# A macaron layer on one core: attention scores as three fp32r products, and four pieces of work moved around them

## The chip, the core and the metric

The kernel runs on one core of a Trainium2 chip. The core has TensorE (matrix products, with its own stream of weight loads), VectorE, ScalarE, GpSimd, and SyncE, which only issues transfers. Each engine takes its instructions in the order in which the program lists them, and waits on semaphores that other engines raise. The metric is the time of one execution in microseconds of the device; lower is better.

## What is computed

The input is `x` of 16 batches x 512 rows x 256 columns. A layer is three residual parts: half a feed-forward network, attention with 16 heads of 64, half the same feed-forward network.

```
x = x + 0.5 * ffn(layernorm(x))
x = x + attention(layernorm(x))
x = x + 0.5 * ffn(layernorm(x))

attention: q, k, v = split(x @ w_qkv); per head
  sim = (q * 64**-0.5) @ k.T - |i - j| * slope(head); causal mask; softmax
  out = sim @ v, heads side by side, @ w_out + b_out
ffn: gelu(x @ w1 + b1) @ w2 + b2
```

## The kernel before

Weights stay in SBUF. Every matmul but two kinds is made of three fp32r products: each operand is split into a high part (the value written as fp32r) and a low part (the value less its high part, written as fp32r), and `hi*hi + hi*lo + lo*hi` is summed in PSUM. The two kinds that use plain fp32 operands are the scores `q @ k.T` and the product of the probabilities with `v`. A plain fp32 matmul shows as two MATMUL records.

Work goes batch by batch. The attention of a batch goes by pairs of heads, c = 0 to 7; I call the pass for one pair a step, and the sixteen records of its scores (before) a block. A block has four parts by row block i, in the order 3, 2, 0, 1 (`QORDER`), of 128(i+1) key columns, and in each part two heads, which use the upper and the lower 64 rows of TensorE. In a step c from 2 on, the engines do this:

- **TensorE**: the block of pair c; the projections k and q of pair c+1 (six products of 512 columns each); a tile of v (twelve products of 256 columns); the product with v of pair c-2 (`values`). In step 6 there are two tiles of v and then the transposes of the next batch's first layer norm (`ln_transpose`, two units of four).
- **ScalarE**: copies of k, q and v out of PSUM (`proj_copy`), the exponentials (`exps`), the copy of `values`.
- **VectorE**: `biased` adds the distances and takes the row minimum, part by part; `inverse` takes reciprocals of the row sums, once for the parts 3 and 2 and once for 0 and 1; `turned` transposes the probabilities of pair c-1 in place, in a large and a small half.
- **GpSimd**: `normalise` multiplies the probabilities by the reciprocals (eight multiplies in two groups of four); then it issues 5 of the 16 transfers that spread the transposed probabilities over the partitions (`spread`). SyncE issues the other 11.

Steps 0 and 1 of a batch stand in `begin`. There TensorE also has the second feed-forward network of the batch before: its up tiles, and its four down tiles `dn(2, b-1, t)`, which VectorE adds to x (`add3`), one by one. Steps are not synchronised otherwise: order on each engine, semaphores, and PSUM banks set the times. Banks are given in turn from a set named by `among`; before a bank is used again, TensorE waits for whoever reads what it held (`bank_free`). Banks 0 to 5 hold scores, bank 5 those of part 1 of the second head. Two places matter here. In step 1, the projection q of pair 2 takes the bank of down tile 1, so it waits for `add3(b-1, 1)`. In step 6 the second unit of transposes takes bank 5, so it waits for `biased(b, 6, 1)`:

```
ln_transpose(1, b + 1, 0)
among[0] = (5,)
ln_transpose(1, b + 1, 1)
```

The next batch's first layer norm has, on VectorE, four `stats` (each a statistics and an aggregate instruction) and a `variance` in step 4, and four `normal` in step 5, all behind the `inverse` at the end of the step; GpSimd takes the power (`power`) in between. `bias` on GpSimd adds a bias to x.

## Time and profile before

| | before |
|---|---|
| time, median of 3 runs (lowest, highest) | 2186.82 us (2186.59, 2187.15) |
| time of the profiled execution | 2185.37 us |
| its span, first to last instruction | 2183.6 us |
| mean granted TensorE clock | 0.995 |
| TensorE matmuls busy | 98% of the span |
| VectorE, ScalarE, GpSimd busy | 69%, 57%, 48% |

The span is what the instructions of the profile cover; 1.8 us of the profiled execution lie around it. Busy shares are of the whole span; matmuls overlap each other in the records, so their starts tell more than their lengths.

### The profile page before, as it was taken

How to read it: one execution, taken by the hardware profiler on the slowest of the kernel's cores; microseconds unless marked ns; L12 is line 12 of the kernel's file. 1: busy time of each engine (PE TensorE's matmuls, PEld its weight loads, DVE VectorE, ACT ScalarE, POOL GpSimd, SP SyncE). 2: the span in 40 equal slices, each digit the busy share in tenths (PEclk: the TensorE clock that was granted, in tenths of full speed). 3: DMA queues.
4: the chain of work that ended last, by engine and by line, in shares of the span. 5: the costliest groups of instructions: out<-in, count | busy, mean ns of one | idle time of the engine just before them, and what ended most of it. 6: DMA issues, size and time to landing. Idle time of an engine off the chain costs nothing.

```text
span 2183.6 us, 41803 instructions
## 1 busy us (share of the span) xinstructions
PE 2138.1 (98%) x14720; PEld 1737.8 (80%) x14720; DVE 1501.8 (69%) x4014; ACT 1234.2 (57%) x3096; POOL 1052.7 (48%) x1770
## 2 busy tenths in 40 slices
PE   7999999999999999999999999999999999999988
PEld 6688787877878788787887878778787787878867
DVE  6766767667676676766768676676766767667664
ACT  5745646466464664736557364564646647465471
POOL 1744627346273553726537174462734537255371
PEclk9999999999999999999999999999999999999998
DMA  3422505234051331514325052250513405143151
GB/s 131 131 73 75 139 1 160 54 90 125 17 149 49 109 104 35 153 27 123 92 62 137 16 141 73 78 135 1 162 52 92 121 23 151 42 115 99 34 146 34
DMA packets 109985, 193.91 MB, mean 89 GB/s; under 512 B 34512, under 2 KB 53200, under 8 KB 109776
## 3 DMA queue, kind: packets, MB, share of 16 engines
q1 hardware_dynamic: 88816, 137.95, 22.5%
q0 software_dynamic: 20480, 52.47, 9.7%
q8 instruction: 117, 1.92, 0.4%
q10 hardware_dynamic: 480, 0.82, 0.1%
q14 instruction: 92, 0.75, 0.1%
HBM read 14.95 MB, written 8.39 MB: 11 GB/s over the span
## 4 chain that ended last, share of the span: by engine, by line
PE 88%; POOL 4%; ACT 4%; DVE 2%; issue 1%; SPq 1%; DMA 0%; DVEq 0%; POOLq 0%
PE ps L302 86%; POOL P L982 3%; PE ps L356 2%; ACT P L629 2%; DVE P L821 1%; ACT L629 1%; SPq L245 1%; POOL PT L245 0%; ACT qk L589 0%; DVE x L768 0%; DMA raw<-in_L_ffn_w 0%; DVE gl L739 0%; DMA PT<-P 0%; DVE P L813 0%; DVE rs L804 0%
## 5 line engine op out<-in xcount | busy, mean ns | idle before, releaser
L982 POOL TENSOR_SCALAR P<-P,rs 128x512 f32<-128x512 f32 (+3 forms) x1024 | 538.5, 543 | 442.9 <-DVE rs L804 439.6
L629 ACT ACTIVATE P<-P,mx 128x512 f32<-128x512 f32 (+3 forms) x1024 | 562.1, 552 | 195.1 <-DVE mx L813 194.9
L245 POOL DMA_DIRECT2D PT<-P x640 | 321.6, 508 | 242.5 <-DVE P L821 228.4
L821 DVE STREAM_TRANSPOSE P<-P 128x1792 f32<-128x1792 f32 (+1 forms) x256 | 374.1, 1486 | 16.2 <-POOL P L982 15.7
L302 PE MATMUL ps<-PT,v 128*64 128x256 f32 (+1 forms) x3072 | 307.5, 349 | 8.5 <-DMA PT<-P 8.4
L302 PE MATMUL ps<-qk 64*128 64x512 f32 (+3 forms) x2048 | 311.0, 443 | 0.7 <-ACT qk L589 0.7
L302 PE MATMUL ps<-w2h,gh 128*128 128x256 f32 x1024 | 292.7, 286 | 0.4 <-DVE gl L739 0.4
L302 PE MATMUL ps<-w2l,gh 128*128 128x256 f32 x1024 | 289.7, 283 | 0.0
L302 PE MATMUL ps<-w2h,gl 128*128 128x256 f32 x1024 | 289.5, 283 | 0.0
L302 PEld LDWEIGHTS ps<-PT,v 128*64 128x64 f32 x3072 | 204.8, 137 | 105.7 <-issue 16.0
L589 ACT ACTIVATE qk<-ps 128x512 f32<-128x512 f32 x256 | 152.7, 597 | 229.9 <-PE ps L302 229.9
L813 DVE CUSTOM_DVE_ANT_1 P<-ps,dist 128x384 f32<-128x384 f32 (+2 forms) x768 | 272.3, 414 | 0.0
L607 ACT ACTIVATE gt<-ps,b1c 128x512 f32<-128x512 f32 x256 | 172.8, 688 | 164.4 <-PE ps L302 130.8
L302 PEld LDWEIGHTS ps<-qk 64*128 64x128 f32 x2048 | 166.2, 187 | 114.9 <-issue 75.8
L813 DVE CUSTOM_DVE_ANT_0 P<-ps,dist 128x512 f32<-128x512 f32 x256 | 165.7, 684 | 122.2 <-PE ps L302 122.2
L768 DVE TENSOR_TENSOR x<-ps,x 128x256 f32<-128x256 f32 x192 | 80.5, 419 | 238.4 <-PE ps L302 236.7
L970 POOL TENSOR_TENSOR rstd<-ve,mhalf 128x4 f32<-128x4 f32 x48 | 62.9, 1310 | 363.2 <-DVE ve L754 363.2
L302 PE MATMUL ps<-xth,wqh 128*128 128x512 f32 x512 | 211.7, 413 | 5.9 <-DVE x L768 4.4
L302 PEld LDWEIGHTS ps<-w2h,gh 128*128 128x128 f32 x1024 | 196.0, 191 | 10.2 <-issue 7.5
L302 PE MATMUL ps<-xtl,wqh 128*128 128x512 f32 x512 | 201.1, 393 | 0.0
L302 PE MATMUL ps<-xth,wql 128*128 128x512 f32 x512 | 199.8, 390 | 0.0
L302 PEld LDWEIGHTS ps<-w2l,gh 128*128 128x128 f32 x1024 | 196.0, 191 | 1.8
(83 smaller groups left out, 4392.4 us busy)
## 6 DMA issues: line engine op xcount, KB each, us to landing
PT<-P SPq DMA_DIRECT2D x1398, 80.0 KB, 2.6
PT<-P POOLq DMA_DIRECT2D x640, 80.0 KB, 2.7
x<-in_L_attn_x SPq DMA_DIRECT2D x16, 512.0 KB, 4.2
out_y<-x SPq DMA_DIRECT2D x15, 512.0 KB, 3.2
raw<-in_L_ffn_w SPq DMA_DIRECT2D x2, 512.0 KB, 5.9
raw<-in_L_ffn_w SPq DMA_DIRECT2D x1, 1024.0 KB, 8.8
rawq<-in_L_attn_w_qkv SPq DMA_DIRECT2D x1, 1024.0 KB, 6.6
rawk<-in_L_attn_w_qkv SPq DMA_DIRECT2D x1, 1024.0 KB, 8.7
```

Source lines behind the costliest of these rows:

```text
L245: e.dma_start(PT[c % 2][32 * m:32 * m + 32, g, :], P[c % 3][32 * g:32 * g + 32, m, :]).then_inc(landed.sem, 16)
L302: return e.matmul(out, lhsT, rhs, start=first, stop=last)
L356: last = e.transpose(dst[:, col:col + 128], xn[:, t, k * 128:(k + 1) * 128], ident[:, :])
L589: e.activation(dst, src, ACT.Copy).then_inc(s_pc.sem, 1)
L607: e.activation(gt[m % 3][:, :], bank_of(("up", f, b, m)), ACT.Gelu, bias=b1c[:, m:m + 1]).then_inc(s_gl.sem, 1)
L629: e.activation(p, p, ACT.Exp, bias=mx[:, r, i:i + 1], scale=-1.0, accum_out=sm[:, r, i:i + 1]).then_inc(s_ex.sem, 1)
L768: e.tensor_tensor(xb[b % 2][:, t, :], bank_of(use)[:, 0:D], xb[b % 2][:, t, :], ALU.add).then_inc(events.sem, 1)
L813: e.tensor_tensor_reduce(out=p_block(c, h, i), in0=score_block(h, i).rearrange("p (m n) -> p m n", m=4), in1=dist[:, :, 128 - 32 * (i + 1) ...
L821: e.transpose(p, p).then_inc(s_tr.sem, 1)
L970: e.tensor_tensor(rstd[:, L - 1, :], ve[:, L - 1, :], mhalf[:, :], ALU.pow).then_inc(s_pw.sem, 1)
L982: e.tensor_scalar(p, p, rs[:, 2 * (c % 2) + h, i:i + 1], 1.0, ALU.mult, ALU.mult).then_inc(s_nz.sem, 1)
```

## The change

- The copies of q and k go to an fp32 buffer `qkf` (for pair 0 of a batch one place, for all others a second). Behind the copy of q, ScalarE writes the high parts of both in one instruction of 1024 elements a partition (`qkh`, one buffer). VectorE's new `qk_lo` writes the low parts, also 1024 elements, over `qkf`. A block then waits for `qk_lo` in place of the copy of q, and each of its parts is three fp32r products for each head. The keys are stored in the order in which the block reads them.
- `qk_lo` of pair c+1 stands in step c behind `biased` of part 0 and ahead of part 1; for pair 0 behind the last `normal` of the batch, for pair 1 behind the gelu splits, for pair 2 behind `add3(b-1, 2)`.
- The next batch's `stats` go to steps 2 and 3 with `variance` in 3, `power` to step 3, and the four `normal` to steps 4 and 5, two each, behind `qk_lo` and ahead of `biased` of part 1.
- `add3(b-1, 1)` goes ahead of `turned(b, 0, 1)`. The copy of k or q now waits for the block just before, not the one two before.
- GpSimd's last `bias` of a batch waits for `qk_lo` of the next batch's pair 0.
- GpSimd issues 6 of the 16 transfers of a spread, SyncE 10; in the last two spreads ScalarE issues 4 in place of 5.

```diff
--- before.py
+++ after.py
@@ -62,7 +62,9 @@
 
     R = at[0]
     QK, V, PP, PT_AT, GT = R, R + 8192, R + 16384, R + 47104, R + 67584
-    qk = [place(f"qk{i}", [128, 2, T], F32, QK + 4096 * i) for i in range(2)]
+    qkh = place("qkh", [128, 2, T], F32R, QK)
+    qkf = [place(f"qkf{i}", [128, 2, T], F32, a) for i, a in enumerate((PP + 10240, QK + 4096))]
+    qkl = [place(f"qkl{i}", [128, 2, T], F32R, a) for i, a in enumerate((PP + 10240, QK + 4096))]
     v = [place(f"v{i}", [128, NT, 4, DH], F32, V + 4096 * i) for i in range(2)]
     P = [place(f"P{i}", [128, 4, GW], F32, PP + 16 * GW * i) for i in range(3)]
     PT = [place(f"PT{i}", [128, 4, GW], F32, PT_AT + 16 * GW * i) for i in range(2)]
@@ -169,6 +171,8 @@
     s_ex = Signal("ex_done", per_block)
     s_pc = Signal("proj_copied", proj)
     s_oa = Signal("out_copied", pairs)
+    s_kh = Signal("qk_hi", pairs)
+    s_kl = Signal("qk_lo", pairs)
     s_lh = Signal("lh_done", units)
     s_gl = Signal("gl_done", hidden)
     s_oh = Signal("oh_done", outs)
@@ -197,12 +201,12 @@
     s_fh = Signal("fh_done", range(NC))
     s_fl = Signal("fl_done", range(NC))
     s_yt = Signal("y_tile_out", range(NT), 16)
-    s_la = {c: Signal(f"spread_last_act{c}", [(NB - 1, c)], 5 * 16) for c in (NC - 2, NC - 1)}
+    s_la = {c: Signal(f"spread_last_act{c}", [(NB - 1, c)], 4 * 16) for c in (NC - 2, NC - 1)}
     s_ls = {c: Signal(f"spread_last_sp{c}", [(NB - 1, c)], 6 * 16) for c in (NC - 2, NC - 1)}
     s_x = Signal("x_in", list(B), 16)
     s_y = Signal("y_out", list(B), 16)
-    s_pt = [Signal(f"spread{i}", [(b, c) for b, c in pairs if c % 3 == i], 11 * 16) for i in range(3)]
-    s_pp = [Signal(f"spread_pool{i}", [(b, c) for b, c in pairs if c % 3 == i], 5 * 16) for i in range(3)]
+    s_pt = [Signal(f"spread{i}", [(b, c) for b, c in pairs if c % 3 == i], 10 * 16) for i in range(3)]
+    s_pp = [Signal(f"spread_pool{i}", [(b, c) for b, c in pairs if c % 3 == i], 6 * 16) for i in range(3)]
     names = ["w1a", "w1b", "b1", "w2", "b2", "wq", "wk", "wv", "wout", "bout"]
     s_w = {n: Signal("in_" + n, [0], 16) for n in names}
 
@@ -230,8 +234,8 @@
         return DH ** -0.5 / SLOPE[h]
 
     GROUPS = [(m, g) for m in range(4) for g in range(4)]
-    SPREAD_SP, SPREAD_POOL = GROUPS[:11], GROUPS[11:]
-    LAST_SP, LAST_ACT, LAST_POOL = GROUPS[:6], GROUPS[6:11], GROUPS[11:]
+    SPREAD_SP, SPREAD_POOL = GROUPS[:10], GROUPS[10:]
+    LAST_SP, LAST_ACT = GROUPS[:6], GROUPS[6:10]
     LAST = (NC - 2, NC - 1)
 
     def spread(e, b, c, groups, landed):
@@ -424,17 +428,20 @@
                 last.then_inc(s_pj.sem, 1)
 
             def scores(b, c):
-                e.wait_ge(s_pc.sem, s_pc.at((b, ("q", c))))
+                e.wait_ge(s_kl.sem, s_kl.at((b, c)))
+                lo = qkl[min(c, 1)]
                 for i in QORDER:
-                    w = 128 * (i + 1)
                     for h in range(2):
                         if i != 0:
                             bank_free(h + {3: 0, 2: 2, 1: 4}[i])
                             held[h + {3: 0, 2: 2, 1: 4}[i]] = ("scores", b, c, 0 if i == 2 else i, h)
-                        hs = slice(64 * h, 64 * h + 64)
-                        keys = qk[c % 2][hs, 1, 0:w].rearrange("p (j m s) -> p m j s", m=4, s=32)
-                        mm(score_block(h, i), qk[c % 2][hs, 0, i * 128:i * 128 + 128], keys,
-                           True, True).then_inc(s_qk.sem, 1)
+                    for n, (q, k) in enumerate(((qkh, qkh), (qkh, lo), (lo, qkh))):
+                        for h in range(2):
+                            hs = slice(64 * h, 64 * h + 64)
+                            keys = k[hs, 1, :].rearrange("p (m n) -> p m n", m=4)[:, :, 0:32 * (i + 1)]
+                            last = mm(score_block(h, i), q[hs, 0, i * 128:i * 128 + 128], keys, n == 0, n == 2)
+                            if n == 2:
+                                last.then_inc(s_qk.sem, 1)
 
             def values(b, c):
                 pv = bank_for(("values", b, c))
@@ -583,10 +590,17 @@
                 else:
                     kind, c = tile
                     n = pairs.index((b, c))
-                    if n >= 2:
-                        e.wait_ge(s_qk.sem, s_qk.at((*pairs[n - 2], QORDER[-1], 1)))
-                    dst = qk[c % 2][:, 0 if kind == "q" else 1, :]
+                    if n >= 1:
+                        e.wait_ge(s_qk.sem, s_qk.at((*pairs[n - 1], QORDER[-1], 1)))
+                    if kind == "q":
+                        dst = qkf[min(c, 1)][:, 0, :]
+                    else:
+                        dst = qkf[min(c, 1)][:, 1, :].rearrange("p (m j s) -> p j m s", m=4, s=32)
+                        src = src.rearrange("p (j m s) -> p j m s", m=4, s=32)
                 e.activation(dst, src, ACT.Copy).then_inc(s_pc.sem, 1)
+                if tile[0] == "q":
+                    e.wait_ge(s_pc.sem, s_pc.at((b, tile)))
+                    e.activation(qkh[:, :, :], qkf[min(c, 1)][:, :, :], ACT.Copy).then_inc(s_kh.sem, 1)
 
             def ln_hi(L, b, u):
                 e.wait_ge(s_lt.sem, s_lt.at((L, b, u)))
@@ -815,6 +829,11 @@
                         in1=dist[:, :, 128 - 32 * (i + 1):128], scale=-SLOPE[2 * c + h],
                         scalar=BIG, op0=ALU.add, op1=ALU.min, accum_out=mx[:, r, i:i + 1]).then_inc(s_tt.sem, 1)
 
+            def qk_lo(b, c):
+                e.wait_ge(s_kh.sem, s_kh.at((b, c)))
+                n = min(c, 1)
+                residue(qkl[n][:, :, :], qkf[n][:, :, :], qkh[:, :, :]).then_inc(s_kl.sem, 1)
+
             def turned(b, c, half):
                 e.wait_ge(s_nz.sem, s_nz.at((b, c, 1, 2 if half else 1)))
                 p = P[c % 3][:, :, HALF[half]]
@@ -825,19 +844,22 @@
                     biased(b, 0, i)
                 if b > 0:
                     gelu_split(2, b - 1, range(NM))
+                qk_lo(b, 1)
+                if b > 0:
                     add3(b - 1, 0)
                 inverse(b, 0, 1)
                 biased(b, 1, 3)
                 biased(b, 1, 2)
                 inverse(b, 0, 0)
-                turned(b, 0, 1)
                 if b > 0:
                     add3(b - 1, 1)
+                turned(b, 0, 1)
                 turned(b, 0, 0)
                 biased(b, 1, 0)
                 biased(b, 1, 1)
                 if b > 0:
                     add3(b - 1, 2)
+                qk_lo(b, 2)
                 inverse(b, 1, 1)
                 if b > 0:
                     add3(b - 1, 3)
@@ -863,17 +885,23 @@
                         turned(b, c - 1, 0)
                     else:
                         turned(b, c - 1, 0)
-                        for i in QORDER[1:]:
+                        for i in QORDER[1:3]:
                             biased(b, c, i)
+                        if c + 1 < NC:
+                            qk_lo(b, c + 1)
+                        if more and c in (4, 5):
+                            normal(1, b + 1, 2 * c - 8)
+                            normal(1, b + 1, 2 * c - 7)
+                        biased(b, c, QORDER[3])
                     inverse(b, c, 1)
-                    if more and c == 4:
+                    if more and c == 2:
                         e.wait_ge(s_x.sem, s_x.at(b + 1))
-                        for t in range(NT):
-                            stats(1, b + 1, t)
+                        stats(1, b + 1, 0)
+                        stats(1, b + 1, 1)
+                    if more and c == 3:
+                        stats(1, b + 1, 2)
+                        stats(1, b + 1, 3)
                         variance(1, b + 1)
-                    if more and c == 5:
-                        for t in range(NT):
-                            normal(1, b + 1, t)
                     if more and c == 6:
                         inverse(b, c, 0)
                         ln_lo(1, b + 1, 0)
@@ -933,6 +961,7 @@
             for u in range(2):
                 ln_lo(2, 0, u)
             split_weight_lo("wv")
+            qk_lo(0, 0)
             e.wait_ge(s_id.sem, s_id.at("dist"))
             for b in B:
                 more = b + 1 < NB
@@ -956,6 +985,8 @@
                 variance(3, b)
                 for t in range(NT):
                     normal(3, b, t)
+                if more:
+                    qk_lo(b + 1, 0)
                 ln_lo(3, b, 0)
                 ln_lo(3, b, 1)
             gelu_split(2, NB - 1, range(NM))
@@ -990,7 +1021,7 @@
                         for h in range(2):
                             normalise(b, c, h, i)
                     if b + 1 < NB:
-                        if c == 4:
+                        if c == 3:
                             power(1, b + 1)
                         if c == NC - 2:
                             bias(1, b + 1)
@@ -1022,6 +1053,8 @@
                     power(2, b + 1)
                     bias(2, b + 1)
                 power(3, b)
+                if b + 1 < NB:
+                    e.wait_ge(s_kl.sem, s_kl.at((b + 1, 0)))
                 bias(3, b)
```

## Rows read from the trace of the kernel before

**Rows 1.** The page, busy time of each engine
```profile
PE 2138.1 (98%) x14720; PEld 1737.8 (80%) x14720; DVE 1501.8 (69%) x4014; ACT 1234.2 (57%) x3096; POOL 1052.7 (48%) x1770
```

**Rows 2.** Timeline, TensorE, one step (start us, us, engine, instruction)
```profile
1010.75 2.43 PE L302 MATMUL ps<-qk 64*128 64x512 f32 x16
1013.10 0.50 PE L302 MATMUL ps<-xth,wqh 128*128 128x512 f32 x1
1013.44 0.40 PE L302 MATMUL ps<-xtl,wqh 128*128 128x512 f32 x1
...
1015.96 0.28 PE L302 MATMUL ps<-wqh,xth 128*128 128x256 f32 x1
...
1017.27 0.28 PE L302 MATMUL ps<-wqh,xtl 128*128 128x256 f32 x1
1017.48 2.38 PE L302 MATMUL ps<-PT,v 128*64 128x256 f32 x24
1019.79 1.13 PE L302 MATMUL ps<-qk 64*128 64x512 f32 x4
```

**Rows 3.** Timeline, TensorE's weight loads, start of one block of scores
```profile
1001.69 0.30 PEld L302 LDWEIGHTS ps<-qk 64*128 64x128 f32 x4
```

**Rows 4.** Groups of instructions by form (count, busy us, mean ns, idle before)
```profile
L739 DVE TENSOR_TENSOR ol<-o,oh 128x1024 fp32r<-128x1024 f32 x60 | 71.9, 1219 | 44.1 <-ACT oh L618 44.1
...
L618 ACT ACTIVATE oh<-o 128x1024 fp32r<-128x1024 f32 x60 | 60.2, 1052 | 40.2 <-PE ps L302 39.7
...
L748 DVE BATCH_NORM_STATS2 st<-x 128x6 f32<-128x256 f32 x192 | 80.0, 417 | 9.3 <-DMA x<-in_L_attn_x 4.9
```

**Rows 5.** Timeline, VectorE, the same step as rows 2
```profile
1011.91 0.69 DVE L813 CUSTOM_DVE_ANT_0 P<-ps,dist 128x512 f32<-128x512 f32 x1 [2.61 <-PE ps L302]
...
1013.13 0.17 DVE L804 RECIPROCAL rs<-sm 128x4 f32<-128x4 f32 x1
1013.22 2.87 DVE L821 STREAM_TRANSPOSE P<-P 128x1792 f32<-128x1792 f32 x2
1016.02 0.52 DVE L813 CUSTOM_DVE_ANT_1 P<-ps,dist 128x384 f32<-128x384 f32 x1
...
1017.37 0.42 DVE L813 CUSTOM_DVE_ANT_1 P<-ps,dist 128x256 f32<-128x256 f32 x1
...
1018.06 0.17 DVE L804 RECIPROCAL rs<-sm 128x4 f32<-128x4 f32 x1
```

**Rows 6.** Timeline, GpSimd, the same step
```profile
1013.40 1.62 POOL L982 TENSOR_SCALAR P<-P,rs 128x128 f32<-128x128 f32 x4 [0.64 <-DVE rs L804]
1016.67 2.50 POOL L245 DMA_DIRECT2D PT<-P  x5 [1.65 <-DVE P L821]
1019.21 2.47 POOL L982 TENSOR_SCALAR P<-P,rs 128x512 f32<-128x512 f32 x4
```

**Rows 7.** Timeline, ScalarE, the same step
```profile
1016.15 0.60 ACT L589 ACTIVATE qk<-ps 128x512 f32<-128x512 f32 x1 [0.76 <-PE ps L302]
```

**Rows 8.** Timeline, VectorE, step 5: first two tiles normalised
```profile
1036.24 0.71 DVE L762 TENSOR_SCALAR xn<-x,mv,rstd 128x256 f32<-128x256 f32 x2
```

**Rows 9.** Timeline, TensorE, step 1: where it waits
```profile
993.68 0.39 PE L302 MATMUL ps<-xth,wql 128*128 128x512 f32 x1
994.36 0.50 PE L302 MATMUL ps<-xth,wqh 128*128 128x512 f32 x1 [0.29 <-DVE x L768]
```

**Rows 10.** Timeline, VectorE, the add that it waits for
```profile
993.92 0.39 DVE L768 TENSOR_TENSOR x<-ps,x 128x256 f32<-128x256 f32 x1
```

**Rows 11.** Timeline, TensorE, down tile 0 and the block behind it
```profile
984.22 0.28 PE L302 MATMUL ps<-w2h,gh 128*128 128x256 f32 x1
...
987.18 0.70 PE L302 MATMUL ps<-qk 64*128 64x512 f32 x2
```

**Rows 12.** Timeline, TensorE, step 6: start of its block, and the transposes
```profile
1037.88 2.43 PE L302 MATMUL ps<-qk 64*128 64x512 f32 x16
...
1045.97 1.04 PE L356 MATMUL ps<-ident,xn 128*128 128x128 f32 x8
```

## Prediction

> **What bounds the kernel now.** I read the page first: TensorE is busy 98% of the span, the next engine 69% [rows 1]. So a microsecond is won only where TensorE gets less to do, and is lost wherever it is made to wait. Then I read TensorE's timeline over one step [rows 2]: block of scores, two projections, a tile of v, `values`, and the next block, 9.04 us later (1019.79 - 1010.75), each tile starting right behind the last. Then the timelines of the other engines over the same step [rows 5 to 7], to see how late each may be before TensorE notices. All times below are counted from the start of the step's block.
>
> **The block gets shorter.** Now it takes 13.10 - 10.75 = 2.35 us, to the start of the projection [rows 2]. For the new one I need the price of an fp32r product. From the second product of the projections to the first of v are 11 products of 512 columns: 2.52/11 = 0.229 us each. From 15.96 to 17.27 are 11 products of 256 columns: 0.119 each [rows 2]. So 0.11 us more for 256 columns more; 384 columns by that line cost 0.174. For 128 columns the line gives 0.065, but a load of weights goes with each product, and where it is not hidden it adds 0.34 - 0.229 = 0.11 (13.10 to 13.44). A product can't be faster than its load, so I take 0.12 for 128 columns too. Two heads: four loads of a block start and end within 0.30 us [rows 3], where four in series would take 0.44 and more, so the two halves of the array load and run side by side, and I count each pair of products once. Three products for each of the four parts: 3 x (0.229 + 0.174 + 0.119 + 0.12) = 1.93; the first load is bare, 0.11; the drain before the next tile is 17.48 - 17.27 - 0.12 = 0.09. New block 2.13 us, 0.22 to 0.23 saved (I use 0.23, from unrounded starts). 16 batches x 8 blocks = 128: **29.4 us** saved if nothing else changes.
>
> Bounds of this price. Below: the slope alone (0.11 per 256 columns) is 0.218 for 512, so 0.011 of each product is a fixed part; if products on half of the array don't have it, and 128 columns cost the bare load of 0.11, the block is about 1.96, 0.40 saved. Above: no fp32r product of fewer than 256 columns is in the trace; if one of 128 costs as much as one of 512, the block is 2.13 + 3 x 0.109 = 2.46, 0.10 lost. I take the middle, as the nearest row is the product of 256 columns.
>
> **What a block now waits for.** ScalarE's copy of q starts at 5.40 and takes 0.60 [rows 7]. All of this comes 0.23 earlier. Then the high parts: 1024 elements, as ScalarE's `oh` copy, 1.05; then the low parts, as VectorE's `ol`, 1.22 [rows 4]. For each handover I take 0.04, an estimate (the add of 993.92 ends at 994.31, TensorE starts again by 994.36 [rows 9, 10]). High parts ready: 5.17 + 0.60 + 0.04 + 1.05 + 0.04 = 6.90; low parts 8.12. The next block is due at 9.04 - 0.23 = 8.81: hidden behind v and `values`, with 0.7 to spare, if VectorE is there on time.
>
> VectorE has the time: its step runs from 11.91 to 18.06 and a reciprocal, 6.25 us [rows 5], and `qk_lo` adds 1.14 (records overlap by 0.08: 1017.37 to 1018.06 is two of 0.42 in 0.69). ScalarE too: it idles 0.76 before q [rows 7], and more elsewhere. But the two run in a ring with GpSimd, and here is the cost.
>
> **The ring.** `normalise` starts 0.27 after the reciprocal (13.13 to 13.40 [rows 5, 6]) and its first four multiplies take 2.47; then the turning, 2.80 to the next instruction; parts 2 and 0, 1.35 (16.02 to 17.37); now `qk_lo` 1.14; in steps 4 and 5 now two `normal`, 0.32 each [rows 8]; part 1, 0.69; the reciprocal again. With `normal` the ring takes 0.27 + 2.47 + 0.04 + 2.80 + 1.35 + 1.14 + 0.64 + 0.69 = 9.40 against a step of 8.81. A second ring, turning 2.87, wake-up and five issues to 19.21 (3.12 after the turning's end at 16.09), one more issue 0.50, multiplies 2.47, takes 9.0. Before, the rings took 7.6 and 8.5 and TensorE led at 9.04.
>
> Followed through: in steps 2 and 3 the second ring loses 0.2 a step, and the moved `stats` (0.42 each and their aggregates [rows 4]) end about where the next part 3 begins. In step 4 `qk_lo` starts at 7.0, the reciprocal at 7.0 + 1.14 + 0.64 + 0.69 = 9.47, the multiplies end at 12.21, and the turning of step 5 starts at 12.25 - 8.81 = 3.44, where VectorE alone would be at 2.3. In step 5 `qk_lo` starts at 3.44 + 2.80 + 1.35 = 7.59 and ends at 8.81, when the block is due: 0.05 lost. The reciprocal is at 10.06, the turning of step 6 at 3.98, `qk_lo` at 8.13, part 1 of the second head ends at 10.03.
>
> **The new wait.** In step 6 the second unit of transposes needs bank 5, so that very part. It came at 1045.97 + 4 x 0.11 - 1037.88 = 8.53 [rows 12], now 8.30. TensorE goes on at 10.03 + 0.04 + 0.11 (a bare load) = 10.18: **1.89 us** of waiting, in 15 batches, with the 0.05 of step 5: 29.1 us. Behind it nothing is late: all that follows in step 7 hangs on TensorE or on VectorE, which are pushed alike.
>
> **Step 1.** TensorE waits before q of pair 2, as `add3(b-1, 1)` stands behind a turning: 994.36 - 993.68 - 0.23 = 0.45, and a bare load, 0.11 [rows 9, 10]. With the add first this goes: the add can start when its tile is ready, about 0.8 before q. But block 1 has only a down tile as cover: copy of q 0.20 after that tile's start at 984.22 (as in rows 2 and 7: 15.96 to 16.15), then 0.60 + 0.04 + 1.05 + 0.04 + 1.22 + 0.04 = 987.41, where the block began at 987.18 [rows 11]: 0.23 lost. Net 0.33 x 15 = 5.0 saved. The exponentials of pair 0 start a microsecond later; the two down tiles before block 2 cover it.
>
> **The first batch** has no down tiles there. Block 1 gets 1.05 + 1.22 + 0.08 = 2.35 more behind q, block 0 about 1.6 more (its tile of v covers the rest): 4.0 lost. Free of charge: GpSimd's `bias`, which stands idle at that place until the first multiplies of the batch; one issue fewer for SyncE, since `values` starts without a wait [rows 2]; the strided copy of the keys, as those of v are no slower. The wait for the next batch's x comes two steps sooner; `stats` stand last in step 2, so only an x that lands later than their place there would hold up VectorE, and the next part 3 with it.
>
> **Sum.** 29.4 + 5.0 - 29.1 - 4.0 = 1.3 us saved of the profiled execution's 2185.37 (span 2183.6 and 1.8 around it), so 2184.1; the median of the runs lies 1.45 above that execution, so **2185.5**. No change, by a measurement that can tell 0.2% (4.4 us).
>
> **Rivals.**
> - *Cheaper products* (0.40 a block). 51.2 + 5.0 - 4.0 saved, but the step is then 8.64, the rings lag sooner, `qk_lo` in step 5 stops the block by 0.5 and step 6 waits 2.1: 15 x 2.6 = 38. Saves 13.9: 2173. For it: the slope. Against it: the fixed part is in every fp32r row there is. The Trainium skill (TensorE: Matmul & The Clock Gate, "Wait — 56ns, not 53.3ns?") gives a fixed part of some 2.5 ns per matmul, which speaks for this rival; the trace has 11 for fp32r.
> - *The rings don't add up*, because the waits overlap better than I chain them. Then `qk_lo` starts in step 6 when the high parts are ready, at 6.90, part 1 ends at 8.80, and the wait is 0.65: 29.4 + 5.0 - 9.8 - 4.0 = 20.7 saved, 2166. Against it: each link is a measured length.
> - *Short products dear*, the other side: one of 128 columns costs what one of 512 does. 128 x 0.10 = 12.8 lost in blocks; the longer step cuts the wait of step 6 to 1.13, 17.0 lost; with + 5.0 and - 4.0, 28.8 lost: 2215.6. It decides from about 0.145 us for 128 columns on. For it: no row excludes it.
> - *Loads not hidden*: each product of a head waits for its own load. The twelve pairs of products stream for 3 x (0.229 + 0.174 + 0.119 + 0.065) = 1.76 and load for 12 x 0.11 = 1.32; with the drain 3.17, 0.82 lost: 105 in blocks, some 9 in step 6: about 2300. Against it: in the projections a load per product is hidden [rows 2]. The Trainium skill (TensorE: Matmul & The Clock Gate, "The mechanism" of packing) says that a load overlaps running matmuls only where their row groups differ; by that rule this rival would hold, and the projections' 0.119 for 256 columns speaks against it.
>
> **How the numbers follow.** The forecast has 0.50; its own range is the wait of step 6 to 0.4 us, 15 x 0.4 = 6: 2179.5 to 2191.5. Cheaper products 0.18, rings that don't add up 0.12, short products dear 0.10, loads 0.06, anything else 0.04. Faster by over 0.2% (below 2182.4): the second and third, and a quarter of the first: 0.42. Slower: dear products, loads, a little of the rest: 0.22. Same: 0.36. The range 2165 to 2212 leaves out the loads, half of the dear products, a third of the rings' case and some of the rest, about 0.18.
>
> **What would show it.** Blocks of 2.13 us; products of 128 columns 0.12 apart; the wait before the second unit of transposes in step 6, put down to VectorE's part 1, at 1.9 us; the turning of steps 5 and 6 beginning at 3.4 and 4.0; no wait before q in step 1 and 0.2 before block 1. I am wrong if the block is not near 2.13, if the transposes don't wait, or if `values` or an up tile does.

## The result, and the profile after

The changed kernel takes 2235.31 us (median of 4 runs, 2233.0 to 2237.1), the kernel before 2186.86: a ratio of 1.0216 with an interval of 1.0204 to 1.0229. The forecast was 2185.5, "no change", with a range up to 2212; the kernel is slower by 48.5 us.

The page of the changed kernel, busy time by engine and then the chain that ended last (the chain of work followed back from the last instruction). The first answers to [rows 1]; the second fence has the chain of the kernel before:

```profile
PE 2121.1 (95%) x15744; PEld 1808.2 (81%) x15744; DVE 1651.8 (74%) x4142; ACT 1368.4 (61%) x3224; POOL 1121.4 (50%) x1898
...
PE 53%; DVE 25%; POOL 5%; DMA 5%; issue 4%; ACT 4%; SPq 4%; DVEq 0%; POOLq 0%; ACTq 0%
```

```profile
PE 88%; POOL 4%; ACT 4%; DVE 2%; issue 1%; SPq 1%; DMA 0%; DVEq 0%; POOLq 0%
```

TensorE is busy 17 us less, but the chain now leaves it for 47% of its length, where it was 12% before. First what went as forecast, a block and its step on TensorE's timeline (batch 4, step 2; it answers to [rows 2]):

```profile
617.77 0.50 PE L306 MATMUL ps<-qkh 64*128 64x512 f32 x2
618.11 0.40 PE L306 MATMUL ps<-qkl,qkh 64*128 64x512 f32 x2
618.34 0.39 PE L306 MATMUL ps<-qkh,qkl 64*128 64x512 f32 x2
618.57 0.34 PE L306 MATMUL ps<-qkh 64*128 64x384 f32 x2
...
619.16 0.28 PE L306 MATMUL ps<-qkl,qkh 64*128 64x128 f32 x2
619.27 0.28 PE L306 MATMUL ps<-qkh,qkl 64*128 64x128 f32 x2
...
619.88 0.50 PE L306 MATMUL ps<-xth,wqh 128*128 128x512 f32 x1
...
624.26 2.38 PE L306 MATMUL ps<-PT,v 128*64 128x256 f32 x24
626.58 0.50 PE L306 MATMUL ps<-qkh 64*128 64x512 f32 x2
```

The block takes 619.88 - 617.77 = 2.11 us (forecast 2.13), the step 8.81. A pair of products of 512 columns costs 0.23, one of 128 columns 0.11. So the gain in the blocks is there, and something else took it. I took the start of every block from the traces; a step is the distance to the next block. Means over batches 1 to 14, in us, for the kernels of this study (the forecast's row is worked out from the typical steps of before and the terms of the prediction):

| kernel | step 0 | 1 | 2 | 3 | 4 | 5 | 6 | 7 | batch | median time |
|---|---|---|---|---|---|---|---|---|---|---|
| before | 19.05 | 14.52 | 9.05 | 9.05 | 9.10 | 9.09 | 11.37 | 52.10 | 133.32 | 2186.86 |
| forecast | 19.05 | 13.72 | 8.81 | 8.81 | 8.81 | 8.86 | 13.02 | 51.85 | 132.93 | 2185.5 |
| **after** | 19.05 | 13.68 | 8.81 | 9.41 | 10.14 | 9.81 | 13.04 | 52.34 | 136.27 | 2235.31 |
| 1 layer norm back | 19.05 | 13.68 | 8.81 | 9.23 | 8.82 | 9.87 | 14.71 | 52.28 | 136.44 | 2240.04 |
| 2 variance of two inputs | 19.05 | 13.68 | 8.81 | 9.36 | 9.99 | 9.81 | 13.13 | 52.30 | 136.12 | 2233.28 |
| 3 variance later | 19.05 | 13.68 | 8.81 | 9.53 | 8.95 | 9.70 | 13.11 | 52.32 | 135.15 | 2217.28 |
| 4 add3 alone | 19.06 | 13.93 | 9.06 | 9.29 | 9.09 | 9.05 | 11.40 | 52.09 | 132.96 | 2180.94 |
| 5 qk_lo(7) late | 19.06 | 13.68 | 8.81 | 9.58 | 8.94 | 9.66 | 12.84 | 52.33 | 134.90 | 2213.30 |
| 6 inverse first | 19.06 | 13.68 | 8.81 | 9.29 | 8.95 | 9.47 | 12.86 | 52.34 | 134.46 | 2208.39 |
| 7 five issues | 19.05 | 13.68 | 8.81 | 9.94 | 9.15 | 9.19 | 12.85 | 52.32 | 135.00 | 2215.84 |
| 8 layer norm a step later | 19.05 | 13.68 | 8.81 | 9.14 | 8.82 | 9.18 | 12.50 | 52.45 | 133.63 | 2197.59 |
| 9 the same, 8 columns | 19.05 | 13.68 | 8.81 | 9.03 | 8.82 | 9.16 | 12.42 | 52.33 | 133.31 | 2193.75 |
| 10 k first | 19.06 | 13.68 | 8.81 | 9.25 | 10.14 | 9.80 | 13.03 | 52.35 | 136.11 | 2236.76 |
| 11 inverse and v | 19.06 | 13.68 | 8.81 | 9.17 | 8.82 | 9.16 | 12.59 | 52.54 | 133.83 | 2194.16 |
| 12 the same, five issues | 19.06 | 13.68 | 8.81 | 9.58 | 8.81 | 8.81 | 12.37 | 52.26 | 133.37 | 2193.26 |
| 13 part 1 first in 6 | 19.05 | 13.68 | 8.80 | 9.53 | 8.81 | 8.83 | 12.15 | 52.55 | 133.41 | 2192.63 |
| 14 x a step later | 19.06 | 13.68 | 8.81 | 8.90 | 8.82 | 8.98 | 12.15 | 52.54 | 132.92 | 2187.46 |
| 15 x later, six issues | 19.05 | 13.68 | 8.81 | 8.93 | 8.82 | 9.20 | 12.29 | 52.52 | 133.29 | 2192.59 |
| 16 both v first | 19.06 | 13.68 | 8.81 | 8.92 | 8.84 | 8.93 | 11.26 | 54.67 | 134.17 | 2205.12 |
| 17 after, step 6 alone | 19.06 | 13.68 | 8.81 | 9.38 | 10.01 | 9.80 | 11.95 | 53.69 | 136.37 | 2237.17 |
| 18 second v between | 19.05 | 13.68 | 8.81 | 8.90 | 8.95 | 9.02 | 11.42 | 53.28 | 133.10 | 2189.52 |

Steps 0 to 2 and 6 of "after" are as forecast. Steps 3, 4 and 5 are longer by 0.60, 1.33 and 0.95, step 7 by 0.49. Three single steps stand out of these means: step 7 of batch 2 takes 54.56 where most take 52.12, step 5 of batches 7 and 12 takes 12.02 and 11.80 where most take 9.46. In or just before each of them GpSimd stood some 2.7 us between two issues, for nothing that the profile shows (batch 7, GpSimd):

```profile
1053.97 1.08 POOL L249 DMA_DIRECT2D PT<-P  x2 [0.65 <-DVE P L840]
1057.76 0.99 POOL L249 DMA_DIRECT2D PT<-P  x2 [2.70 <-issue]
```

The other batches lose as well, and what was late there is on VectorE's timeline (batch 4, from the end of step 2 to part 3 of step 4):

```profile
628.18 0.43 DVE L762 BATCH_NORM_STATS2 st<-x 128x6 f32<-128x256 f32 x1 [1.51 <-DMA x<-in_L_attn_x]
...
629.32 0.69 DVE L827 CUSTOM_DVE_ANT_0 P<-ps,dist 128x512 f32<-128x512 f32 x1
...
637.66 0.18 DVE L764 BATCH_NORM_AGGREGATE mv<-st 128x2 f32<-128x6 f32 x1
637.88 1.76 DVE L768 TENSOR_SCALAR ve<-mv 128x4 f32<-128x4 f32 x1
639.54 0.68 DVE L827 CUSTOM_DVE_ANT_0 P<-ps,dist 128x512 f32<-128x512 f32 x1
```

First, the stats wait 1.51 us for x, so part 3 of step 3 begins 629.32 - 626.58 = 2.74 us behind its block, where batch 15, which has no next layer norm, has 1.0. SyncE's queue says why x is late: its load waits until the store of y has landed.

```profile
619.90 0.58 SPq L268 DMA_DIRECT2D out_y<-x  x1
623.08 0.38 SPq L260 DMA_DIRECT2D x<-in_L_attn_x  x1
623.56 5.83 SPq L249 DMA_DIRECT2D PT<-P  x9
```

Second, the variance, an instruction over 4 elements, takes 1.76 us and ends as GpSimd's four multiplies do, 637.12 + 2.49 = 639.61 (GpSimd's timeline):

```profile
637.12 2.49 POOL L1013 TENSOR_SCALAR P<-P,rs 128x512 f32<-128x512 f32 x4
```

So part 3 of step 4 begins 3.48 behind its block. Behind it ScalarE has its exponentials and then the copy of k, and every later link of the step moves with it. (Beside GpSimd's multiplies the variance isn't always so slow; the last section has its row in the kernel before.) The list of waits shows where TensorE feels it (us in total, times, longest):

```profile
PEld ps L306 <- DVE qkl L753: 37.1, 63, 3.5
PEld ps L306 <- ACT qkf L600: 30.4, 27, 2.1
...
DVE st L762 <- DMA x<-in_L_attn_x: 22.7, 14, 4.7
```

### The profile page after: what moved, and what is told of

The parts are those of the page before. It is cut to its first block, busy times and chain, and to the rows that moved or that the text cites. A ratio compares the mean times of both kernels' runs of the same rounds, so it can differ in the third digit from the quotient of the medians.

```text
span 2233.1 us, 44380 instructions
## 1 busy us (share of the span) xinstructions
PE 2121.1 (95%) x15744; PEld 1808.2 (81%) x15744; DVE 1651.8 (74%) x4142; ACT 1368.4 (61%) x3224; POOL 1121.4 (50%) x1898
## 4 chain that ended last, share of the span: by engine, by line
PE 53%; DVE 25%; POOL 5%; DMA 5%; issue 4%; ACT 4%; SPq 4%; DVEq 0%; POOLq 0%; ACTq 0%
PE ps L306 52%; DVE P L840 10%; DVE P L827 6%; POOL P L1013 4%; DVE qkl L753 4%; SPq L249 4%; DMA x<-in_L_attn_x 3%; DMA out_y<-x 2%; ACT qkh L603 2%; PE ps L360 2%; DVE xn L776 1%; ACT qkf L600 1%; DVE st L762 1%; POOL PT L249 1%; ACT P L643 1%
## 5 line engine op out<-in xcount | busy, mean ns | idle before, releaser
L249 POOL DMA_DIRECT2D PT<-P x768 | 388.7, 512 | 227.3 <-DVE P L840 208.6
L827 DVE CUSTOM_DVE_ANT_1 P<-ps,dist 128x384 f32<-128x384 f32 (+2 forms) x768 | 278.3, 415 | 0.2 <-PE ps L306 0.2
L600 ACT ACTIVATE qkf<-ps 128x512 f32<-128x512 f32 x256 | 149.7, 593 | 158.1 <-PE ps L306 158.1
L753 DVE TENSOR_TENSOR qkl<-qkf,qkh 128x1024 fp32r<-128x1024 f32 x128 | 156.6, 1223 | 63.1 <-ACT qkh L603 61.5
L306 PE MATMUL ps<-qkh 64*128 64x512 f32 (+3 forms) x1024 | 179.4, 347 | 24.0 <-DVE qkl L753 24.0
L306 PEld LDWEIGHTS ps<-w2h,gl 128*128 128x128 f32 x1024 | 196.1, 192 | 0.0
L643 ACT ACTIVATION_READ_ACCUMULATOR P<-P,mx 128x1 f32 x1024 | 193.8, 189 | 0.0
```

What stands on the lines that cost most here:

```text
L249: e.dma_start(PT[c % 2][32 * m:32 * m + 32, g, :], P[c % 3][32 * g:32 * g + 32, m, :]).then_inc(landed.sem, 16)
L306: return e.matmul(out, lhsT, rhs, start=first, stop=last)
L600: e.activation(dst, src, ACT.Copy).then_inc(s_pc.sem, 1)
L643: e.activation(p, p, ACT.Exp, bias=mx[:, r, i:i + 1], scale=-1.0, accum_out=sm[:, r, i:i + 1]).then_inc(s_ex.sem, 1)
L753: return e.tensor_tensor(dst, src, hi.bitcast(F32), ALU.subtract)
L827: e.tensor_tensor_reduce(out=p_block(c, h, i), in0=score_block(h, i).rearrange("p (m n) -> p m n", m=4), in1=dist[:, :, 128 - 32 * (i + 1) ...
```

## The experiments

Theory T: the moved layer norm makes VectorE late in steps 2 to 5. Theory R: the ring through `qk_lo`, the multiplies, the turning and six issues is the loss wherever the layer norm stands. Intervals of the ratio to the kernel before are in brackets.

**1. Layer norm back.** `stats` and `variance` in step 4, `normal` in step 5, behind the inverse, as before the change (the cut shows the new places; the lines at the old ones go).

```
-                    if more and c == 2:   # stats 0, 1; c == 3: stats 2, 3, variance
+                    if more and c == 4:   # wait for x, stats 0 to 3, variance
+                    if more and c == 5:   # normal 0 to 3
```

> The changed kernel with the next batch's layer norm back at its old place: the four stats and the variance behind the inverse of step 4, the four normals behind the inverse of step 5, the power in step 4. The three products, the order of b2's adding, the 10 and 6 issues and add3 stay. Theory T (the moved layer norm makes part 3 late on VectorE, and by ScalarE's order k and the v tile): steps 3 and 4 fall from 9.41 and 10.14 to 8.81 and about 9.0, step 5 (9.81) to about 9.5, step 6 stays at about 13.0, so some 2 us a batch, 30 in all: about 2205 us. Theory R (the ring through qk_lo and GpSimd's issues is the loss wherever the layer norm stands): steps 4 and 5 stay near 10 and the time within 8 us of 2235.

2240.04 (1.0225 to 1.0255). Neither: step 4 came down as T has it and step 3 in part (9.23), but step 6 rose to 14.71. Beside `qk_lo` the old place costs as much as the new one. VectorE and GpSimd in step 5 of batch 4:

```profile
657.03 3.79 DVE L776 TENSOR_SCALAR xn<-x,mv,rstd 128x256 f32<-128x256 f32 x4
```

```profile
657.55 2.48 POOL L1010 TENSOR_SCALAR P<-P,rs 128x512 f32<-128x512 f32 x4
```

The first normal takes 0.38, the second 2.84: it ends when the fourth multiply does. So another instruction is held as the variance was.

**2 and 3. Two ways around the hold.** Run 2 computes the variance by another form at the same place; run 3 moves it.

```
-                e.tensor_scalar(ve[:, L - 1, :], mv[:, L - 1, :, 1], EPS, None, ALU.add)
+                e.scalar_tensor_tensor(ve[:, L - 1, :], mhalf[:, :], -2.0 * EPS, mv[:, L - 1, :, 1], ALU.mult, ALU.add)
```

```
                         biased(b, c, 3)
+                        if more and c == 4:
+                            variance(1, b + 1)
                         inverse(b, c - 1, 0)
```

> The changed kernel with the variance computed by another form of instruction at the same place: mhalf (-0.5) times -2 EPS plus the variance, from two tiles, in place of one tile plus a constant. Theory T1 (a tensor_scalar on VectorE that starts while GpSimd multiplies is held until GpSimd ends, and the other form is not): its duration falls from 1765 ns to about 0.2 us, part 3 of step 4 begins at about 1.9 us behind its block in place of 3.48, step 4 falls from 10.14 to about 9.0 to 9.4, and the time to some 2218 to 2225 us. Theory T2 (any small instruction is held there): the duration stays near 1.77 us and the time at 2235.

> The changed kernel with the variance moved from behind stats 2 and 3 in step 3 to behind part 3 of step 4, where GpSimd has ended its multiplies and only issues DMAs or waits. If GpSimd's multiplies hold it (T1, T2 alike), it takes about 0.2 us there, part 3 of step 4 begins some 1.5 us sooner, and the time falls to some 2218 to 2225 us. If the variance is slow for a reason of its own, it takes 1.77 us there as well, in front of the inverse and the turning, and the time is at 2235 or above.

2233.28 (1.0193 to 1.0228) and 2217.28 (1.0117 to 1.0150). The variance by its tile in run 2, then in run 3 (count, shortest/median/longest ns):

```profile
L770 DVE SCALAR_TENSOR_TENSOR ve<-mhalf,mv x48: 161/164/1736, 7.0 to 2197.5; 128x4 f32<-128x4 f32 x48
```

```profile
L768 DVE TENSOR_SCALAR ve<-mv x48: 169/170/596, 7.1 to 2184.9; 128x4 f32<-128x4 f32 x48
```

The form with two inputs is held just as long. Behind part 3 of step 4 GpSimd hasn't ended its multiplies yet, though the expectation has it so: the variance still meets the last of the four and ends with it, but that makes it 0.6 at the most. Step 4 falls by 1.19, which is 16.7 in 14 batches, and the time by 18.0 against 2235.31 (the four runs spread from 2211.5 to 2220.3). So that hold alone is about a third of the loss.

**4. `add3` alone**, in the kernel before.

```
+                if b > 0:
+                    add3(b - 1, 1)
                 turned(b, 0, 1)
-                if b > 0:
-                    add3(b - 1, 1)
```

> The kernel before with one edit: add3(b-1,1) ahead of turned(b,0,1) in step 1, scores as one product. If the wait of 0.56 us that [rows 9] shows in step 1 goes and nothing takes its place, step 1 falls from 14.52 to about 13.96 in 15 batches: 2178.4 us (8.4 less). If the turning that is later by one addition is itself waited for (by the DMAs and the values of step 1), step 1 stays at 14.52 and the time at 2186.8.

2180.94 (0.9955 to 0.9981): the fastest kernel of the study. Step 1 gains 0.59 as forecast, but step 3 gives 0.24 of it back: in batch 2 it takes 10.04, since `values` start at 350.25, behind a copy of v on ScalarE that ends at 350.20. Why that copy is late in some batches I didn't follow.

**5 to 7. One link of the ring each**, from run 3: `qk_lo(b, 7)` behind the inverse of step 6; the inverse ahead of part 1; 11 and 5 issues in place of 10 and 6.

```
-                        if c + 1 < NC:
+                        if c + 1 < NC and not (more and c == NC - 2):
                             qk_lo(b, c + 1)
...
+                    if more and c == NC - 2:
+                        qk_lo(b, NC - 1)
```

```
+                        inverse(b, c, 1)
                         biased(b, c, QORDER[3])
-                    inverse(b, c, 1)
```

```
-    SPREAD_SP, SPREAD_POOL = GROUPS[:10], GROUPS[10:]
+    SPREAD_SP, SPREAD_POOL = GROUPS[:11], GROUPS[11:]
```

> The kernel of the later variance (2217.3), with qk_lo(b,7) in step 6 behind part 1 and the inverse in place of ahead of part 1; the score block that needs it comes 13 us behind that of step 6. Step 6 (13.11) holds two waits of the next batch's transposes: the first for the v copy that ScalarE has behind the exponentials of part 2, the second for the bank that part 1 gives back. If only the second goes by qk_lo(7), step 6 falls by about 0.5 to 12.6 and the time to about 2209; if the whole 1.7 that step 6 has gained over before is qk_lo(7)'s, step 6 falls to about 11.4 and the time to 2192; if the low parts of the last pair are then late for block 7 or hold up the next batch's low parts, the time stays at 2217 or rises.

> The kernel of the later variance (2217.3), with the inverse of parts 3 and 2 ahead of part 1 on VectorE, so that GpSimd's multiplies start some 0.8 us sooner behind qk_lo. Theory R1 (the chain qk_lo, normals, part 1, inverse, multiplies, turning, parts 2 and 0, qk_lo sets steps 5 and 6): step 5 (9.70) falls to about 9.0 and the lag into step 6 is less, 0.7 to 1.2 us a batch, 2200 to 2207 us. Theory R2 (GpSimd's own chain of six issues, four multiplies and the turning sets them): 9.0 us a step stays, and since the inverse was early enough there, the time stays within 4 us of 2217.

> The kernel of the later variance (2217.3), with the issues of the turned tiles shared 11 and 5 as in the kernel before, in place of 10 and 6. By R2, GpSimd's chain shortens by one issue of 0.49 us: steps 5 and 6 fall by 0.3 to 0.5 each, about 2205 us. By R1, GpSimd waits for VectorE anyway: within 4 us of 2217, or some us above if SP's eleventh issue makes the values late.

2213.30 (1.0107 to 1.0137), 2208.39 (1.0084 to 1.0114) and 2215.84 (1.0114 to 1.0147), against 2217.28. The inverse first gave 8.9, with step 5 at 9.47, between the expectation's theories R1 and R2. `qk_lo(b, 7)` late gave 4.0, which the spread of run 3 doesn't tell from nothing, though step 6 fell by 0.27. Five issues shortened steps 5 and 6 by 0.51 and 0.26, as R2 has it, lengthened steps 3 and 4 by 0.41 and 0.20, and left the time as it was.

**8. Layer norm a step later**, from run 5: stats in steps 3 and 4, variance behind part 3 of step 5, normals in 5 and 6.

```
-                        if more and c in (4, 5):   # normal 2c-8, 2c-7
+                        if more and c in (5, 6):   # normal 2c-10, 2c-9
-                    if more and c == 2:            # wait for x, stats 0, 1; c == 3: 2, 3
+                    if more and c == 3:            # wait for x, stats 0, 1; c == 4: 2, 3
```

> The kernel with qk_lo(7) late, with each part of the next batch's layer norm one step later: stats 0 and 1 in step 3, stats 2 and 3 in step 4, the variance behind part 3 of step 5, the normals in steps 5 and 6, the power in step 4's turn on GpSimd. If the wait for x in step 2 is what makes steps 3 and 4 long, step 3 falls from 9.5 to about 8.85 and the time by about 10 us against the kernel with qk_lo(7) late. If VectorE's added work itself (2.1 us of stats over two steps with 0.7 us to spare in each) makes them long, step 4 and 5 take over what step 3 gives up, and the time stays within 4 us of it; if the normals in step 6 are late for the transposes, step 6 grows by about 1 us and the time by 15.

2197.59 (1.0036 to 1.0066), 15.7 below run 5. Steps 4 and 5 are at 8.81 in most batches, step 3 is still long in some, and step 6 fell by 0.34 though it now has two normals in it.

**9. What the layer norm's length is worth**, from run 8: from batch 1 on, the statistics and the four normals take 8 of 256 columns; the rest of that computation is left out. (Cut; `normal` has the same edit.)

```
+                n = 8 if L == 1 and b > 0 else D
-                e.bn_stats(st[:, L - 1, t, :], xb[b % 2][:, t, :])
+                e.bn_stats(st[:, L - 1, t, :], xb[b % 2][:, t, 0:n])
```

> The kernel with each part of the layer norm a step later (2197.6), with the next batch's stats and normals computed over 8 of 256 columns (that part of the computation is left out), the same instructions in the same places. What VectorE's time in them is worth: by theory T (VectorE, with some 8.1 of 8.81 us taken in each step, has no room for the layer norm's 3.9 us and hands the lag on into step 6) step 6 falls from 12.50 to about 11.5 and the time by 12 to 20 us, to 2178 to 2186. By theory R (the low parts and GpSimd's chain alone make step 6 long) step 6 stays above 12.2 and the time at 2193 or more.

2193.75 (1.0020 to 1.0042): step 6 at 12.42. So once the layer norm stands a step later, its length is not what makes step 6 long, as R has it. A stats with its aggregate still takes 0.27 us there and a normal 0.29, so this took only some 1.5 us of VectorE's time from a batch.

**10. k first**, from the changed kernel.

```
-                    exps(b, c, 3)
                     if c + 1 < NC:
                         proj_copy(b, ("k", c + 1))
+                    exps(b, c, 3)
```

> The changed kernel with one edit in ScalarE's order: from step 2 on, the copy of k(c+1) ahead of the exponentials of part 3 of step c in place of behind them. If a late part 3 reaches TensorE through ScalarE's order (theory T's middle link), the waits of the v tile for k's copy (0.8 to 1.5 us in steps 3 and 4) go: step 4 falls from 10.14 to 9.3 to 9.6, step 3 by some 0.3, and the time to about 2220 to 2227. If the late qk_lo holds the next block just as long, steps 3 and 4 stay as they are and the time within 4 us of 2235; if the exponentials are now late for the multiplies, it rises.

2236.76 (1.0215 to 1.0246): step 4 stays at 10.14, so the first reading missed. The order on ScalarE is where TensorE's wait is booked, but without it `qk_lo`, itself behind the late turning, holds the next block just as long: in batch 4 the wait of 1.12 for the copy goes and the block of step 5 waits 1.22 for `qk_lo`.

**11 and 12. Inverse and v**, from run 8: the inverse first, and in step 6 ScalarE's copy of the first v tile ahead of the exponentials of part 2; run 12 with five issues.

```
+                    if more and c == NC - 2:   # step 6: first v tile here
                     exps(b, c, 2)
-                    for tile in steps_v(b, c)[:1]:
```

> The kernel with each part of the layer norm a step later (2197.6), with the inverse of parts 3 and 2 ahead of part 1 as in the run with the inverse first, and in step 6 the copy of the v tile ahead of the exponentials of part 2 on ScalarE. The inverse shortens VectorE's chain by 0.77 us a round, so the turning of step 6 starts nearer 2.8 than 3.5 us; the v copy takes the first of step 6's two waits (1.27 us) away, and then the second, for the bank of part 1, sets the end. Step 6 falls from 12.50 to 11.7 to 12.0 and the time to 2186 to 2191. If the second wait only grows by what the first loses, and the inverse gives nothing, it stays at 2197.

> The same with the issues shared 11 and 5 between SP and GpSimd as in the kernel before. GpSimd's chain is shorter by one issue of 0.49 us, so that the turnings no longer fall back by 0.2 us a step: another 0.2 to 0.4 us of step 6, 4 to 6 us below the kernel with 10 and 6. If SP's eleventh issue makes the values of steps 3 and 4 late, as step 3 of the first run with 11 and 5 had it (9.94 against 9.53), it is even or some us above.

2194.16 (1.0021 to 1.0049) and 2193.26 (1.0017 to 1.0038), less than expected. In run 12 steps 4 and 5 are clean, but step 3 has 9.58. SyncE's queue in batch 3, and then TensorE:

```profile
480.02 0.38 SPq L260 DMA_DIRECT2D x<-in_L_attn_x  x1
480.49 10.94 SPq L249 DMA_DIRECT2D PT<-P  x13
```

```profile
490.09 1.26 PE L306 MATMUL ps<-PT,v 128*64 128x256 f32 x9 [0.82 <-DMA PT<-P]
```

SyncE stands at the load of x until y's store has landed, the issues of pair 1 start late, and `values` of step 3 waits for them.

**13. Part 1 first in step 6**, from run 12; **14. x a step later**, from run 13; **15**, run 14 with ten and six issues. (The expectation of 15 speaks of run 11 with x alone changed; its edit has part 1 first in step 6 as well, so it compares cleanly with run 14.)

```
+                        if c != NC - 2:
                             inverse(b, c, 1)
                         biased(b, c, QORDER[3])
+                    if c == NC - 2:
+                        inverse(b, c, 1)
```

```
-                    if c == 0 and b + 1 < NB:
+                    if c == 1 and b + 1 < NB:
                         load_x(b + 1)
```

> The kernel with the inverse first, v first in step 6 and 11 and 5 issues (2193.3), with one edit: in step 6 alone part 1 goes ahead of the inverse again. There the inverse waits for the exponentials of part 2 and holds part 1 back by 1.1 us, and the second transposes wait 1.30 us for part 1's bank. If that order is the cause, step 6 falls from 12.37 to 11.2, what before has less the shorter scores, and the time by 17 us to 2176. If the chain of low parts, turning and issues is the cause, another wait takes its place (the normals, the copies of x's transposes) and step 6 stays above 12.0, the time above 2188.

> The same with the next batch's x loaded behind the spread of step 1's pair in place of step 0's, so that SP no longer stands for 2.7 us at the load of x (it waits for the store of y) in front of the 11 issues of the turned tiles of pair 1. If that makes step 3 long in some batches (mean 9.58), step 3 falls to 8.85 and the time by 10 us to about 2166. If x then lands too late for the stats of step 3, part 3 of step 4 is late and step 4 grows by as much; if SP's 11 issues alone are the cause, step 3 stays at 9.5.

> The kernel with the inverse first, v first in step 6, 10 and 6 issues and the inverse ahead of part 1 in all steps (2194.2), with x loaded a step later as well. It has step 6 at 12.4 (12.59 in that run) and shows x's place alone: step 3 falls from 9.17 to 8.85 and the occasional 10.9 to 11.3 of step 5 stays, about 2188; if x lands too late for the stats, step 4 grows and the time stays at 2194.

2192.63 (1.0020 to 1.0039), 2187.46 (0.9996 to 1.0015) and 2192.59 (1.0020 to 1.0039). With x later, step 3 falls to 8.90 as expected, the time by 5.2, half of what was expected. Between runs 14 and 15 the issues alone differ, and the sixth costs 5.1. Run 15's long steps are above all those of batches 2, 5, 7 and 12 in or just before which GpSimd stands 2.5 to 2.75 us between two issues, as in every kernel with six. Kernels with five have such stops too, but four of the five are in step 7, where they cost the kernel before at most 0.2. Step 6 fell only to 12.15: in run 14 the transposes no longer wait long, but `values` behind them does:

```profile
1317.20 0.66 PE L360 MATMUL ps<-ident,xn 128*128 128x128 f32 x4 [0.20 <-DVE mx L832]
1318.39 2.38 PE L306 MATMUL ps<-PT,v 128*64 128x256 f32 x24 [0.54 <-ACT v L600]
```

**16. Both v first**, from run 14; **17. Step 6 alone**, from the changed kernel with `qk_lo(7)` late and both v first; **18**, the second v between the exponentials of parts 2 and 0.

```
+                    if more and c == NC - 2:
+                        vs = [steps_v(b, c), [], []]   # run 18: [first, second, none]
+                    for tile in vs[0]:
+                        proj_copy(b, tile)
                     exps(b, c, 2)
```

> The kernel with x loaded a step later (2187.5), with both v copies of step 6 ahead of the exponentials of part 2 on ScalarE, in place of the first alone. If the second v copy is the last wait of step 6, step 6 falls from 12.15 to about 11.15 and the time by 15 us to about 2172, below the kernel before. If the exponentials, 0.6 us later, hold the inverse, the turning and the values of step 7 instead, step 7's stretch (52.5) grows by as much and the time stays at 2187.

> The changed kernel with two edits, both in step 6: qk_lo(b,7) behind part 1 and the inverse, and both v copies ahead of the exponentials of part 2. The layer norm stays where the change put it, in steps 2 to 5. If these orders make step 6 long, it falls from 13.04 to 12.0 to 12.3 (part 1 still ends late, since the turning of step 6 starts at 4.0 us) and the time by 11 to 15 us, to 2220 to 2224. If the late turning is all of it, step 6 stays at 12.8 or more and the time at 2231 or more.

> The kernel with x loaded a step later (2187.5), with the second v copy of step 6 between the exponentials of part 2 and those of part 0. If the inverse of parts 3 and 2 is what the chain of pair 6 hangs on, it isn't delayed: step 6 falls from 12.15 to 11.4 to 11.7, step 7's stretch stays at 52.5 and the time falls by 6 to 10 us to 2178 to 2182. If the later exponentials of parts 0 and 1 delay the turning as well, step 7's stretch rises by what step 6 gives and the time stays within 4 us of 2187.5.

2205.12 (1.0073 to 1.0100), 2237.17 (1.0221 to 1.0239) and 2189.52 (1.0003 to 1.0021). In all three step 6 gave what was asked, and step 7 took as much or more back. TensorE in step 7, run 16 and then run 17:

```profile
1343.41 0.87 PE L306 MATMUL ps<-PT,v 128*64 128x256 f32 x6 [1.75 <-DMA PT<-P]
```

```profile
1366.30 1.05 PE L306 MATMUL ps<-PT,v 128*64 128x256 f32 x7 [1.34 <-DMA PT<-P]
```

And VectorE in run 16, where the inverse of pair 6 waits for the exponentials that the v copies delayed, so the turning and its transfers come later:

```profile
1326.37 0.18 DVE L823 RECIPROCAL rs<-sm 128x4 f32<-128x4 f32 x1 [1.54 <-ACT P L643]
...
1330.04 2.04 DVE L845 STREAM_TRANSPOSE P<-P 128x1792 f32<-128x1792 f32 x1
```

Steps 6 and 7 together: 65.38 after, 65.64 in run 17, 64.69 in run 14, 65.93 in run 16, 64.70 in run 18, and 63.47 before. In batch 9 the product with v of pair 6 starts 26.47 behind the block of step 6 in run 17 and 26.13 in the changed kernel, though run 17's step 6 is 1.15 shorter there. So it looks as if the chain of pair 6 sets the two steps, whatever waits in step 6.

## Why the prediction was wrong

**The block, right.** 2.11 against 2.13, and the price of short products with it (0.11 against 0.12). (The lower bound of that price was summed wrongly: 3 x (0.218 + 0.163 + 0.108 + 0.11) + 0.11 + 0.09 is 2.00, not 1.96. The forecast doesn't use it.) The rival of loads not hidden falls: the rule of the Trainium skill (TensorE: Matmul & The Clock Gate, "The mechanism" of packing), that a load overlaps running matmuls only where row groups differ, doesn't hold for these rows (pairs of 256 columns stand 0.12 apart and pairs of 128 columns 0.11, each product with a load of its own).

**Step 1, right.** 13.68 against 13.72; run 4 shows the add's part by itself, 0.59 against 0.56.

**"The moved `stats` ... end about where the next part 3 begins", wrong.** This step failed first, in two terms. I named x's landing as the only danger and gave it no price, though the transfer's path (y's store, its landing, then x's load of 5 us) was in the trace; it landed 1.5 us late in the batch shown. And I let the variance pass at no cost: it took 0.2 us at its old place and takes 1.76 at the new one, beside GpSimd's multiplies. The trace of before had a sign that such holds exist. I read the first two normals, 0.71 together [rows 8], while the tile view there gave, for all of them:

```profile
L762 DVE TENSOR_SCALAR xn<-x,mv,rstd x192: 382/409/2030, 8.9 to 2152.8; 128x256 f32<-128x256 f32 x192
```

A longest of five times the median asks what ran beside it. The Trainium skill (SBUF — State Buffer, "Who interferes with whom") has the rule: VectorE's copies and tensor_scalar, and its instructions with two SBUF inputs, can contend with GpSimd for a shared port pair, and whoever is second waits for the whole instruction of the first. Runs 1 to 3 agree as to which instructions are held, the form with two inputs included; how long they are held (1.76 and 2.84 us, more than one multiply) goes beyond it. By runs 3 and 8, standing otherwise gives 18.0 + 15.7 = 33.7 of the 48.5 back. The old place isn't that better place: run 1 stands at 2240.04.

**"Followed through", wrong by what it left out.** The lengths of the two rings were right: in batch 15 the turning falls back by 0.23 a step, as 9.04 against 8.81. But the ring was followed from an undisturbed step 3. With part 3 of step 4 at 3.48, the turning of step 5 begins at 4.0, not 3.44; step 5 is 9.46 in most batches, where I had 8.86. The turning of step 6 begins at 4.0 all the same (forecast 3.98), since the longer step 5 took the lag in: that this number came out is luck.

**One more issue, mis-sized.** I gave it 0.50 in the second ring. GpSimd's stops between two issues are in the trace of before (2.5 to 2.7 us, at five places), and with six issues they come at other places: the three steps named above lose 7.3 us, and runs 14 and 15 put the sixth issue at 5.1.

**The new wait of step 6: the size right, the cause half.** 13.04 against 13.02. TensorE in batch 4:

```profile
664.96 0.66 PE L360 MATMUL ps<-ident,xn 128*128 128x128 f32 x4 [1.23 <-ACT v L600]
665.86 0.66 PE L360 MATMUL ps<-ident,xn 128*128 128x128 f32 x4 [0.24 <-DVE mx L827]
```

Most of it stands before the first unit, for a bank that ScalarE's v copy gives back, behind late exponentials; the rest before the second, for part 1, where I had all 1.89. In run 5, where part 1 is no longer behind `qk_lo`, the copy of v alone leaves step 6 at 12.84; that the two together come to my number is in part luck. **"Behind it nothing is late", wrong**, and hidden by the wait: run 17 took 1.09 out of step 6 and `values` of pair 6 waited 1.34.

**Step 7, one place left out.** `qk_lo` of the next pair 0 stands ahead of the low part of the last layer norm and delays it: the second transposes stand 2.37 us behind the first (at 1402.11), where before it was 2.07 (1098.66 to 1100.73). The rest of step 7's 0.49 is in two batches (54.56 and 52.62). Batch 9, VectorE, then TensorE:

```profile
1402.60 1.23 DVE L753 TENSOR_TENSOR qkl<-qkf,qkh 128x1024 fp32r<-128x1024 f32 x1 [0.64 <-ACT qkh L603]
1403.74 0.69 DVE L753 TENSOR_TENSOR x3l<-ps,x3h 128x512 fp32r<-128x512 f32 x1
```

```profile
1404.48 0.66 PE L360 MATMUL ps<-ident,xn 128*128 128x128 f32 x4 [0.34 <-DVE x3l L753]
```

**The first batch, mis-sized.** Its first block comes 2.48 later (53.25 against 50.77) and it takes 123.14 against 116.60: 9.0 lost on the whole. The prediction's terms give 4.1 (4.0 and the wait of step 6, 1.9, less eight blocks of 0.23).

**The sum.** Against the forecast a batch lost 136.27 - 132.93 = 3.34, in 14 batches 46.8; the first batch 4.9 more, the last batch 1.3 more. Less 2.0 of strays in the batches of before (133.32 where most have 133.18, 14 times), that is 51.0; the span is 2233.1, and the forecast's was 2184.1 - 1.8, a difference of 50.8.

What stays open: with the layer norm in a good place (run 14) the shorter scores and the moved add win 1.6 us a batch in steps 0 to 5, and steps 6 and 7 lose 1.2 of it, the first batch 9 us once, so the whole is no change. That pair 6's chain through the low parts is what sets those two steps is argued from runs 16 to 18 and not shown: each of them also delays exponentials of pair 6, and a kernel with shorter low parts was not tried. Nor is it shown why GpSimd stops between two issues.

## What to carry to other kernels

Before a small instruction is moved, look at what runs beside its new place, and at the longest of its group as well as the mean: a 0.2 us instruction cost 18 us here. A short time at the old place is no promise for the new one, even beside the same neighbour. A wait that disappears at one place has to be followed to the next consumer of the same chain; three orders of step 6 each removed a wait and moved it into step 7. Edits that come together should be run alone: of this change the one moved add is worth 6 us, and it is the best kernel of the study.
